# Three steps of the score bound behind each V-projection tile in place of two, in a fused layer norm, attention and feed-forward kernel on eight cores

## The chip, the cores and the metric

The kernel runs on all 8 cores of one Trainium2 chip. Each core takes one half (1024 queries) of the sequence of one of four batch items; the cores don't exchange data. The time is device microseconds of the slowest core. The profile is one execution on the slowest core (core 7).

## The reference

```python
xn = _layernorm(x)                                   # x: (4, 2048, 2048)
# attention on xn: a second layer norm, then
qkv = einsum('bsd,df->bsf', Xn, W_in)                # 16 heads of 128
Q, K = _rope(Q), _rope(K)                            # first 64 channels rotated in pairs
probs = softmax(Q K^T / sqrt(128))
attn = einsum(probs V, W_out) + X
# feed-forward on xn, weights dequantized: (w - 128) * scale
h = silu(xn Wg^T) * (xn Wu^T)                        # 8192 wide
out = x + attn + h Wd^T
```

## The kernel before

The program is a list of operations for each engine, written in the order in which each engine runs them; an operation waits on counters of the operations that it needs. An engine never passes a waiting operation, so the order of the list is the order of the work. There are four stages: layer norms with transposes (`_emit_ln`), attention (`_emit_attention`), output projection, feed-forward.

Attention runs over eight groups `g` of two heads each. In a group, TensorE first makes the projections of Q (4 tiles) and K (8 tiles, each 128x512, 16 matmuls). Behind each of them ACT copies the tile out of its PSUM bank and the rotary embedding of the previous tile follows (`rope`): one matmul into `ppR` (L497) and three DVE operations, a product with the cosine (L501), one with the sine out of PSUM (L505) and their addition (L508). The rotary embedding of the last K tile is left pending and is emitted behind the matmuls of the first V tile.

Then comes the V projection: 16 tiles `tb`, each of 16 matmuls 128x256 (L604), in four PSUM banks in rotation, each copied out by ACT (L611). Beside it the kernel works out, for each head, an upper bound of the scores, which becomes the bias of the exponential. This work is the list `bsteps`, 11 steps a head, 22 a group, in the order

- `s_sq("q",0)`: POOL squares 1024 columns of Q into the buffer `sqb` (L533); it waits for `sq_free`, the last product of the head before,
- `s_mm(0)`, `s_mm(1)`: TensorE sums the squares over the partitions with a matrix of ones (L549) into the bank `j % 3` of S, D0, D1; DVE reduces one row of the bank to its maximum (L555), and the bank is free again behind that (`bankF`),
- `s_sq("k",0)`, `s_mm(2)`, `s_mm(3)`: the same for the first half of K. The square (L538) waits for the last product emitted (`state["mb"]`), since `sqb` is overwritten,
- `s_sq("k",1)`, `s_mm(4)`, `s_mm(5)`: the second half of K,
- `s_fin`: four small DVE operations on the six maxima (L567, L569, L571, L573), a matmul that spreads the value over the partitions (L576), and a copy of it into `biasc` (L579),
- a step that emits nothing and sets `sq_free` for the next head.

Some steps are emitted behind the matmuls of each V tile until the list is empty. Behind the V projection come the loads and POOL casts of the next group's weights (`load_slab`, L444) and then the attention of the group's two heads, whose exponentials wait for `bias_ready` and whose first score matmul waits for the last V tile.

Of the kernel before, what the change touches and what calls it, by code (L numbers as in the profile page):

```python
# [115 lines left out]
def build_program(stage=STAGE, debug=DEBUG):  # L116
# [45 lines left out]
    with ExitStack() as top:  # L162
# [23 lines left out]
        with ExitStack() as sCtx:  # L186
          env["sCtx"] = sCtx
          with ExitStack() as sA:
            env["xn2"] = sA.enter_context(nc.sbuf_tensor("xn2f", [128, ND * S], BF16, side="left"))
            env["cs"] = sA.enter_context(nc.sbuf_tensor("cs_sb", [128, S], F32, side="left"))  # L190
            ldc = []
            for i, (name, dst) in enumerate([
                    ("lnwc", env["lnw"]), ("lnbc", env["lnb"]),
                    ("gscp", env["gsc"]), ("uscp", env["usc"]),
                    ("pmat", env["pm"]), ("idf", env["idf"]),
                    ("cs", env["cs"])]):
                prog.dma("sync", lambda e, d=dst, s=dram[name]: e.dma_start(out=d[:, :], in_=s[:, :]),
                         sem=f"ldc{i}")
                ldc.append((f"ldc{i}", 16))
            env["ldc"] = ldc  # L200
            for dst, valc in [(env["ones_cb"], 1.0), (env["ones_bb"], 1.0), (env["ones_rf"], 1.0),
                              (env["n128"], -128.0), (env["eps_c"], EPS)]:
                prog.op("vector", lambda e, d=dst, vv=valc: e.memset(d[:, :], vv))
            env["dvc_done"] = prog.v("vector")

            _emit_ln(env, xb)
            if debug:
                prog.barrier()
                prog.dma("sync", lambda e: e.dma_start(out=dram["d_xn2"][:, :], in_=env["xn2"][:, :]), sem="st")
                prog.dma("sync", lambda e: e.dma_start(out=dram["d_xnfm"][:, :], in_=env["xnfm"][:, :]), sem="st")  # L210
                prog.dma("sync", lambda e: e.dma_start(out=dram["d_rstd"][:, :], in_=env["rstd"][:, :]), sem="st")
                prog.dma("sync", lambda e: e.dma_start(out=dram["d_nmr"][:, :], in_=env["nmr"][:, :]), sem="st")

            if stage >= 2:
                _emit_attention(env)
                if stage == 2:
                    prog.barrier()
# [167 lines left out]
def _emit_attention(env):  # L385
# [12 lines left out]
    with ExitStack() as ctx:  # L398
# [56 lines left out]
        for g in range(8):  # L455
# [140 lines left out]
            for tb in range(NT):  # L596
                sl = tile_i % 4
                w0 = [("gpsimd", slab_ready[slabv])] + pp_free[sl] + v2_rd
                if g == 0:
                    w0 += env["x2ev"][tb]  # L600
                v2_rd = []
                m_last = None
                for dc in range(ND):
                    m_last = prog.op(T, lambda e, d=dc, t=tb, s=sl, sj=slabv: e.matmul(  # L604
                                         pp4[s][:, 0:256],
                                         xn2f[:, d * S + t * 128: d * S + t * 128 + 128],
                                         wbf[sj % 3][:, d * 256: d * 256 + 256],
                                         start=(d == 0), stop=(d == ND - 1)),
                                     waits=(w0 if dc == 0 else ()))
                wbf_mm_last[slabv % 3] = m_last  # L610
                aev = prog.op(Sc, lambda e, s=sl, t=tb: e.activation(  # L611
                                  v2[:, t * 256:(t + 1) * 256], pp4[s][:, 0:256], AF.Copy),
                              waits=[(T, m_last)])
                vproj_last = aev
                if pending_rope is not None:
                    pending_rope()
                    pending_rope = None
                pp_free[sl] = [(Sc, aev)]
                tile_i += 1
                for _ in range(2):  # L620
                    if bi < len(bsteps):
                        bsteps[bi]()
                        bi += 1
# [554 lines left out]
```

How the kernel before makes its waits and increments, by code:

```python
            def body(eng):  # L89
                for fn, waits, eseq, dsem in ops:
                    if fn == "BARRIER":
                        if e == "sync":
                            eng.sem_inc(sems["bar"], 1)
                        else:
                            eng.drain().then_inc(sems["bar"], 1)
                        eng.wait_ge(sems["bar"], waits)
                        continue
                    for wname, wval in waits:
                        if wname in ENGS:
                            eng.wait_ge(sems["q" + wname], rank[wname][wval])
                        else:
                            eng.wait_ge(sems[wname], wval)
                    inst = fn(eng)
                    if dsem is not None:
                        inst.then_inc(sems[dsem], 16)
                    if eseq in marks:
                        inst.then_inc(sems["q" + e], 1)
```

## Time and profile before

| what | value |
|---|---|
| median of 2 runs | 2918.7 us (2917.88 to 2919.51) |
| profiled execution | 2913.32 us |
| span of the profile, core 7 | 2911.8 us |
| spans of the eight cores | 2901.7 to 2911.8 us |
| mean granted TensorE clock by core | 0.953 to 0.960 |
| V projections of the eight groups | about 291 us to 1267 us, one each 133 to 134 us |

The span runs from the first to the last instruction of a core. PE is TensorE, PEld its weight loads, DVE VectorE, ACT ScalarE, POOL GpSimd. The ends of matmuls are modelled, so the distance between two starts is a better measure than an end. A wait is put down to the operation whose semaphore came last.

### The profile page before, as it was taken

To read this page: it belongs to the slowest core of one execution; us is meant where nothing else is said; L and a number is where in the kernel's file an instruction comes from. 1 tells how busy PE (TensorE), PEld (TensorE's weight loads), DVE (VectorE), ACT (ScalarE), POOL (GpSimd) and SP (SyncE) were. 2 spreads that over 40 slices of the span, in tenths; PEclk is the share of its full clock that TensorE was granted. 3 is DMA by queue.
4 is the path that set the end of the run, shared out by engine and by line. 5 is a ranking of instruction groups with operands and counts; after the bars stand their busy time and mean duration, and the time that the engine had idled before them with its cause. 6 is when DMAs were issued, how large, how long until landed. Compare 5 with 4: busy or idle time off the path is not lost.

```text
span 2911.8 us, 37331 instructions; the slowest of 8 cores (2901.7 to 2911.8 us)
## 1 busy us (share of the span) xinstructions
PE 2590.6 (89%) x12552; PEld 1239.5 (43%) x12552; DVE 633.5 (22%) x1012; ACT 770.8 (26%) x1282; POOL 475.5 (16%) x436
## 2 busy tenths in 40 slices
PE   3537898999999898986979999989998999998996
PEld 2223544445453535442434444434443444443443
DVE  5753352424334342422000000001110000000111
ACT  4572526161625344251111111110001111110000
POOL 2242302121121203000011111110011111110010
PEclk9758999999999999997989999999999999999998
DMA  4113202020211202004133333335544333333553
GB/s 132 59 58 95 87 1 88 1 87 15 74 37 51 62 26 80 1 1 166 66 138 151 145 145 145 145 131 183 182 163 148 148 145 145 145 145 135 186 174 112
DMA packets 64490, 305.61 MB, mean 105 GB/s; under 512 B 7732, under 2 KB 7860, under 8 KB 40632
## 3 DMA queue, kind: packets, MB, share of 16 engines
q1 hardware_dynamic: 55096, 286.45, 27.9%
q10 hardware_dynamic: 9216, 16.78, 1.8%
q8 instruction: 112, 1.84, 0.3%
q14 instruction: 66, 0.54, 0.1%
HBM read 294.81 MB, written 8.39 MB: 104 GB/s over the span
## 4 chain that ended last, share of the span: by engine, by line
PE 85%; DMA 4%; POOL 3%; issue 3%; DVE 3%; ACT 1%; SPq 0%; ACTq 0%; DVEq 0%; POOLq 0%
PE pg L917 15%; PE pu L935 15%; PE pg L990 8%; PE pu L990 8%; PE pp L476 6%; PE ppC L476 6%; PE po L797 4%; PE pp L604 4%; PE ppC L664 4%; PE ppD L672 3%; PE pst L343 3%; PE pp L646 2%; PE ppC L604 2%; POOL sqb L538 2%; PE ppR L497 1%
## 5 line engine op out<-in xcount | busy, mean ns | idle before, releaser
L917 PE MATMUL pg<-xnfm,wstage 128*128 128x512 bf16 x2048 | 465.8, 381 | 18.6 <-ACT sgp L926 12.3
L935 PE MATMUL pu<-xnfm,wstage 128*128 128x512 bf16 x2048 | 464.6, 380 | 2.6 <-DMA wstage<-ubp 2.6
L947 POOL TENSOR_TENSOR hfm<-sgp,sup 128x512 bf16<-128x512 f32 x128 | 161.7, 1264 | 996.2 <-ACT sup L943 996.2
L917 PEld LDWEIGHTS pg<-xnfm,wstage 128*128 128x128 bf16 x2048 | 200.8, 98 | 264.0 <-issue 24.7
L935 PEld LDWEIGHTS pu<-xnfm,wstage 128*128 128x128 bf16 x2048 | 200.8, 98 | 245.7 <-issue 5.3
L926 ACT ACTIVATE sgp<-pg,gsc_sb 128x512 f32<-128x512 f32 x128 | 88.0, 688 | 614.8 <-PE pg L917 344.9
L990 PE MATMUL pg<-wstage,hfm 128*128 128x512 bf16 x1024 | 231.4, 383 | 14.0 <-DMA wstage<-dwp 14.0
L657 ACT ACTIVATE ebig<-pp,biasc 128x512 bf16<-128x512 f32 x344 | 228.7, 687 | 30.3 <-PE pp L646 26.0
L990 PE MATMUL pu<-wstage,hfm 128*128 128x512 bf16 x1024 | 227.7, 379 | 0.0
L967 DVE CAST hsr<-phs 1x512 bf16<-1x512 f32 x2 | 1.4, 679 | 913.0 <-PE phs L956 913.0
L664 PE MATMUL ppC<-ebig,v 128*128 128x512 bf16 x448 | 169.6, 379 | 26.8 <-ACT ebig L657 26.7
L476 PE MATMUL pp<-xn2f,wbf 128*128 128x512 bf16 x768 | 173.9, 381 | 17.1 <-POOL wbf L444 16.8
L943 ACT ACTIVATE sup<-pu,usc_sb 128x512 f32<-128x512 f32 x128 | 88.0, 687 | 373.9 <-PE pu L935 373.9
L697 DVE RECIPROCAL rb<-ppD 128x512 f32<-128x512 f32 x32 | 107.4, 3357 | 351.7 <-PE pp L646 195.8
L343 PE MATMUL pst<-idf_sb,xn2t 128*128 128x128 f32 x256 | 68.8, 365 | 127.1 <-POOL xn2t L320 126.9
L476 PE MATMUL ppC<-xn2f,wbf 128*128 128x512 bf16 x768 | 174.1, 380 | 0.0
L672 PE MATMUL ppD<-ebig,ones_bb 128*128 128x512 bf16 x448 | 169.7, 379 | 0.0
L444 POOL CAST wbf<-wf 128x512 bf16<-128x512 f32 x192 | 118.9, 621 | 250.7 <-DMA wf<-wip 239.7
L990 PEld LDWEIGHTS pg<-wstage,hfm 128*128 128x128 bf16 x1024 | 99.8, 99 | 137.6 <-issue 22.7
L990 PEld LDWEIGHTS pu<-wstage,hfm 128*128 128x128 bf16 x1024 | 98.9, 98 | 120.7 <-issue 3.6
L797 PE MATMUL po<-wob,ctxf 128*128 128x512 bf16 x512 | 113.3, 385 | 28.9 <-DVE wob L781 28.9
L646 PE MATMUL pp<-q,k 128*128 128x512 bf16 x344 | 126.4, 379 | 5.0 <-ACT v L611 5.0
(103 smaller groups left out, 2298.5 us busy)
## 6 DMA issues: line engine op xcount, KB each, us to landing
wstage<-gbp SPq DMA_DIRECT2D x64, 1024.0 KB, 4.9
wstage<-ubp SPq DMA_DIRECT2D x64, 1024.0 KB, 7.0
wstage<-dwp SPq DMA_DIRECT2D x32, 2048.0 KB, 8.9
wf<-wip SPq DMA_DIRECT2D x192, 256.0 KB, 2.9
xt<-xb SPq DMA_DIRECT2D x16, 1024.0 KB, 9.8
wof<-wop SPq DMA_DIRECT2D x8, 2048.0 KB, 9.8
xst<-xb ACTq DMA_DIRECT2D x32, 256.0 KB, 5.3
out<-out_acc ACTq DMA_DIRECT2D x32, 256.0 KB, 3.3
```

What stands on the lines that cost most here:

```text
L343: mm_t = prog.op(T, lambda e, sb=srcbuf, d=dc, pp=p: e.transpose(pp[:, 0:128], sb[:, d * 128:(d + 1) * 128], idf[:, :]), waits=wts)
L476: m_last = prog.op(T, lambda e, d=dc, h=hh, t=tg, s=sl, sj=slabj: e.matmul(pp4[s][:, :], wbf[sj % 3][:, d * 256 + h * 128: d * 256 + (h + ...
L604: m_last = prog.op(T, lambda e, d=dc, t=tb, s=sl, sj=slabv: e.matmul(pp4[s][:, 0:256], xn2f[:, d * S + t * 128: d * S + t * 128 + 128], wb ...
L646: ms_seq[kb] = prog.op(T, lambda e, h=hh, q=qg, k=kb, s=sl: e.matmul(pps[s][:, :], k2[:, h * 2048 + k * 128: h * 2048 + (k + 1) * 128], q2 ...
L657: ex_seq[kb] = prog.op(Sc, lambda e, k=kb, s=sl, h=hh: e.activation(ebig[:, (k % 8) * 512:(k % 8) * 512 + 512], pps[s][:, :], AF.Exp, bias ...
L664: prog.op(T, lambda e, k=kb - 2, h=hh, u=un: e.matmul(ppC[u][:, :], v2[:, k * 256 + h * 128: k * 256 + (h + 1) * 128], ebig[:, (k % 8) * 5 ...
L672: md_seq[kb - 2] = prog.op(T, lambda e, k=kb - 2, u=un: e.matmul(ppD[u][:, :], ones_bb[:, :], ebig[:, (k % 8) * 512:(k % 8) * 512 + 512], ...
L797: m_last = prog.op(T, lambda e, hh=h, t=tb, s=sl, q=wp: e.matmul(po[s][:, :], ctxf[:, hh * 1024 + t * 128: hh * 1024 + (t + 1) * 128], wob ...
L917: m = prog.op(T, lambda e, h=hc, i2=ic2, p=par, t=tg, s=psl: e.matmul(pg[s][:, :], gb2[p][:, h * 256 + i2 * 128: h * 256 + i2 * 128 + 128] ...
L935: m = prog.op(T, lambda e, h=hc, i2=ic2, p=par, t=tg, s=psl: e.matmul(pu[s][:, :], ub2[p][:, h * 256 + i2 * 128: h * 256 + i2 * 128 + 128] ...
L947: gh = prog.op(G, lambda e, i=ic: e.tensor_mul(hfm[:, i * 512:(i + 1) * 512], sgp[:, :], sup[:, :]), waits=[(Sc, a2), (Sc, a1), (T, h_free)])
L990: m = prog.op(T, lambda e, f=fg, p=pc, q=par, t=tb, i=icp: e.matmul(pd[t][:, :], hfm[:, (p * 16 + i) * 512 + t * 128: (p * 16 + i) * 512 + ...
```

## The change

One number: the loop behind each V tile emits up to three steps of `bsteps` in place of two. The steps, their order among themselves and their waits are the same; on every engine they come to stand earlier relative to the V tiles.

```diff
--- before.py
+++ after.py
@@ -617,7 +617,7 @@
                     pending_rope = None
                 pp_free[sl] = [(Sc, aev)]
                 tile_i += 1
-                for _ in range(2):
+                for _ in range(3):
                     if bi < len(bsteps):
                         bsteps[bi]()
                         bi += 1
```

The loop that holds it, with its neighbours:

```python
aev = prog.op(Sc, ... v2[:, t*256:(t+1)*256], pp4[s][:, 0:256], AF.Copy ...)
if pending_rope is not None:
    pending_rope()
    pending_rope = None
pp_free[sl] = [(Sc, aev)]
tile_i += 1
for _ in range(2):            # 3 after the change
    if bi < len(bsteps):
        bsteps[bi]()
        bi += 1
```

## Rows read from the trace of the kernel before

**Rows 1.** The page: busy us (share of the span) and instructions of each engine.

```profile
PE 2590.6 (89%) x12552; PEld 1239.5 (43%) x12552; DVE 633.5 (22%) x1012; ACT 770.8 (26%) x1282; POOL 475.5 (16%) x436
```

**Rows 2.** Waits of PE: waiting line <- releaser: us in total, times, longest.

```profile
PE ppS L576 <- DVE scr L573: 25.3, 16, 2.5
PE ppD L549 <- POOL sqb L538: 16.9, 32, 0.6
```

**Rows 3.** Windows, L604 alone: length, busy us of PE and PEld (x), clock, DMA.

```profile
415.00:470.00 55.00, 29.75 (x256) 24.50 (x256) 1.00 0.16 49
548.00:603.00 55.00, 32.66 (x256) 25.98 (x256) 0.94 0.15 46
...
815.00:870.00 55.00, 31.18 (x256) 25.22 (x256) 0.97 0.14 39
...
sum 440.00, PE 248.60 PEld 201.39; mean PE 31.08 PEld 25.17
```

**Rows 4.** Timeline, PE, third group, behind the long wait for the bias.

```profile
571.57 3.60 PE L604 MATMUL pp<-wbf,xn2f 128*128 128x256 bf16 x16
```

**Rows 5.** Timeline, PE, sixth group: start, us, instruction, [idle before <-releaser].

```profile
961.67 0.39 PE L549 MATMUL ppS<-sqb,ones_bb 128*128 128x512 bf16 x1
...
963.65 0.38 PE L549 MATMUL ppD<-sqb,ones_bb 128*128 128x512 bf16 x1
...
966.32 0.38 PE L549 MATMUL ppD<-sqb,ones_bb 128*128 128x512 bf16 x1 [0.55 <-POOL sqb L538]
966.55 0.38 PE L549 MATMUL ppS<-sqb,ones_bb 128*128 128x512 bf16 x1
...
971.20 0.38 PE L549 MATMUL ppD<-sqb,ones_bb 128*128 128x512 bf16 x1
974.13 0.35 PE L576 MATMUL ppS<-scr,ones_rf 1*128 1x1 f32 x2 [2.55 <-DVE scr L573]
974.41 1.92 PE L604 MATMUL pp<-wbf,xn2f 128*128 128x256 bf16 x16
976.16 1.91 PE L604 MATMUL ppC<-wbf,xn2f 128*128 128x256 bf16 x16
...
985.45 0.61 PE L549 MATMUL ppD<-sqb,ones_bb 128*128 128x512 bf16 x2 [0.55 <-POOL sqb L538]
...
988.46 0.35 PE L576 MATMUL ppS<-scr,ones_rf 1*128 1x1 f32 x2 [0.63 <-DVE scr L573]
988.74 0.50 PE L604 MATMUL ppC<-wbf,xn2f 128*128 128x256 bf16 x3
```

**Rows 6.** Timeline, all engines, second group, end of the first head's steps.

```profile
435.88 0.38 PE L549 MATMUL ppD<-sqb,ones_bb 128*128 128x512 bf16 x1
...
436.40 1.89 POOL L533 TENSOR_TENSOR sqb<-q 128x1024 bf16<-128x1024 bf16 x1 [2.89 <-PE ppD L549]
...
437.64 0.67 DVE L571 TENSOR_TENSOR scr<-scr 1x1 f32<-1x1 f32 x1
```

**Rows 7.** Line L571: duration ns min/median/max, first and last start.

```profile
L571 DVE TENSOR_TENSOR scr<-scr x16: 148/406/666, 304.9 to 1256.9; 1x1 f32<-1x1 f32 x16
```

**Rows 8.** Chain of work that ended last, second group: start, us, what.

```profile
438.56 0.24 issue
```

**Rows 9.** Timeline, all engines, fourth group, around tile 0.

```profile
693.83 0.39 PE L549 MATMUL ppS<-sqb,ones_bb 128*128 128x512 bf16 x1
...
694.01 0.68 DVE L501 TENSOR_TENSOR k<-k,cs_sb 64x512 bf16<-64x512 bf16 x1
...
695.49 0.68 DVE L508 TENSOR_TENSOR k<-k,rb 64x512 bf16<-64x512 bf16 x1
...
696.10 0.67 DVE L555 TENSOR_REDUCE scr<-ppS 1x1 f32<-1x512 f32 x1
```

**Rows 10.** Timelines of POOL and DVE, second group: a square meets a product.

```profile
391.57 1.89 POOL L533 TENSOR_TENSOR sqb<-q 128x1024 bf16<-128x1024 bf16 x1 [30.45 <-DVE q L508]
...
393.09 0.92 DVE L501 TENSOR_TENSOR q<-q,cs_sb 64x512 bf16<-64x512 bf16 x1 [1.72 <-PE ppR L497]
```

## The prediction

> **What bounds the kernel now.** I read the page first: TensorE is busy for 89% of the span and every other engine for less than a third [rows 1]. So time is won or lost where TensorE waits or its clock falls. The change touches only the V projection of each of the eight groups, so I then read the waits of PE. Two entries belong to the interleaved steps [rows 2]: the square products (`s_mm`, L549) wait 32 times for a POOL square, 16.9 us in all, and the bias matmul (`s_fin`, L576) waits 16 times for a chain of small DVE operations, 25.3 us in all. 42 us of 2912 is everything these steps cost as waits. The third view is the windows of the V-projection matmuls group by group [rows 3]: 29.75 us busy where the granted clock is 1.00, up to 32.66 where it fell. The eight groups sum to 248.60, so 248.60 - 8 x 29.75 = 10.6 us go to stretches at the lower of the clock's two levels (1.2 GHz against 2.4), in five of the eight groups (granted clock 0.94 or 0.97 over the window). The timeline of one such group shows where [rows 4]: the tile just behind the long bias wait takes 3.60 us instead of 1.92. The fourth view, the timeline of PE in the sixth group, gives the positions on which I count [rows 5].
>
> **What the change moves.** Nothing is removed or added. There are 22 steps a group (11 a head: q square, two products, k square, two products, k square, two products, fin, close). Two a tile fill tiles 0 to 10; three a tile fill tiles 0 to 7. What can cost is how many V tiles lie between a step and the one that feeds it. I name the products of a head mm0 to mm5 and mark those of the second head with a prime.
>
> Before, by tile: 0 sq mm0; 1 mm1 sq; 2 mm2 mm3; 3 sq mm4; 4 mm5 fin; 5 close sq'; 6 mm0' mm1'; 7 sq' mm2'; 8 mm3' sq'; 9 mm4' mm5'; 10 fin' close.
> After: 0 sq mm0 mm1; 1 sq mm2 mm3; 2 sq mm4 mm5; 3 fin close sq'; 4 mm0' mm1' sq'; 5 mm2' mm3' sq'; 6 mm4' mm5' fin'; 7 close.
>
> A k square is released by a TensorE product, not by its place in TensorE's stream, so the distances are mm1 to mm2 and mm3 to mm4, and they are one V tile before and after, in both heads. This is my first result: the four POOL waits of a group stay. Each is 966.32 - 963.65 = 2.67 us from mm1 to mm2, against 0.22 for the product and 1.75 for the tile (976.16 - 974.41): 0.70 lost [rows 5].
>
> The first q square runs during the Q and K tiles in either version. The second head's waits for mm5 and has two tiles before mm0', before and after.
>
> The bias matmul swaps heads. Before, fin sits right behind mm5 in tile 4 and waits in full: 974.13 - 971.20 = 2.93 us, 2.71 of them lost beyond the product's 0.22. fin' has a tile in front: 988.46 - 985.45 = 3.01 us from mm4', less two products (0.44) and a tile (1.75), 0.8 lost [rows 5]. After, fin has the tile and fin' has none. The second result is that one fin stays naked.
> fin': mm4' to bias again 3.01, less 0.44, is 2.57 lost, 0.14 less than the naked one before.
> fin: here the q square of the second head runs on POOL beside DVE's chain. It starts 0.52 us after mm5 (436.40 - 435.88) and ends at 438.29; the tiny addition L571 starts at 437.64 and ends at 438.31, 0.67 us where the fastest of its kind takes 0.148 [rows 6, 7]. So DVE's addition waits for POOL's square to end. After: mm5 is at 0.22 behind mm4, the square ends at 0.22 + 0.52 + 1.89 = 2.63, the addition at 2.65, the next scalar operation 0.1 + 0.14 later, then 0.25 to TensorE (issue row, [rows 8]): 3.14 from mm4, less 2.19, 0.95 lost.
>
> **The new wait, in tile 0.** mm1 moves from behind tile 1 to directly behind mm0, and the k square with it, into the time in which DVE still works on the last rotary embedding (three operations, `rope`). Let T be the start of mm0, 693.83 [rows 9]. DVE's first rope product runs T+0.18 to T+0.86, the addition `k<-k,rb` (two SBUF inputs) T+1.66 to T+2.34, and the reduction of mm0's bank T+2.27 to T+2.94. Today the square comes after all that (mm1 is at T+1.97, the square 0.5 later). After: mm1 at T+0.22, POOL wants to start at T+0.74. If the first rope product holds it off, T+0.87; it ends at T+2.63 to T+2.76. The addition then meets a running square. Its price is read from another such meeting [rows 10]: POOL's square ends at 393.46, DVE's SBUF-SBUF product ends at 394.01, 0.55 later. So the addition ends at T+3.31 instead of T+2.34, the reduction runs T+3.24 to T+3.91, and mm3, which needs bank S back (`bankF`), may start 0.25 later, at T+4.16. mm2 is ready at T+2.76+0.26 = T+3.02, so mm3 could have been at T+3.24: 0.92 lost, and mm2 itself loses 0.12 more than now. Behind mm3 everything on TensorE queues: tile 2, the next k square, fin. Nothing on another engine is that late that it would hide this. Bounds: if the addition isn't held, mm3 waits only to T+2.94+0.25 = T+3.19 against T+3.12, 0.07 lost; if the reduction were put off by the whole square (1.89 in place of 0.97), 1.9. I take 0.92 because both meetings in the trace show a DVE operation with two SBUF inputs ending with or after POOL's square.
> No row shows the other direction, a POOL square that finds DVE at work; the 0.12 is between nothing and the 0.12 by which the first rope product outlasts T+0.74, and I keep it.
> The Trainium skill, "SBUF — State Buffer", section "Who interferes with whom", has a rule for both directions: a DVE operation with two SBUF inputs and a GpSimd operation that reads SBUF exclude each other, and whichever comes second waits for the whole of the first. By that rule the group comes out at +0.99; with DVE's side of it alone it would be +0.87, and without either at the lower bound. For DVE's side this case's trace agrees (0.67 against 0.148 us [rows 6, 7]); for POOL's side no run here shows it yet.
>
> **Sum of a group at full clock**, from mm0: mm1 0.22; tile 1 0.44 to 2.19; mm2 3.02; mm3 4.16; tile 2 to 6.13; mm4 6.83; mm5 7.05; tile 3 to 9.02; fin 9.97; tile 4 10.25 to 12.00; mm0', mm1', tile 5 12.43 to 14.18; mm2' 14.88; mm3', tile 6 to 17.07; mm4' 17.77; fin' 20.78; tile 7 at 21.06; four tiles later tile 11 at 28.06. Before, the same stretch is 988.74 - 961.67 = 27.07 [rows 5]. Difference +0.99 us a group, +7.9 us for eight. By parts: +0.12 + 0.92 (tile 1) + (0.95 + 2.57) - (2.71 + 0.82) = 1.03, the same within rounding. POOL's casts of the next weights start some 5 us earlier, since the last square is three tiles earlier; nobody waits for them but the next group, so they cost nothing. Bias values are ready earlier too, but their reader, the first exponential of attention, waits for the last V tile.
>
> **The clock.** The naked fin wait stays about as long (2.57 against 2.71 lost) but comes two tiles later and directly behind the wait of mm4'. I leave the 10.6 us as they are. Bounds: 0 if the clock never falls there; 8 x 2.9 = 23.3 if it falls in each group as in the worst one (32.66 - 29.75 = 2.91 [rows 3]), that is -10.6 to +12.7.
>
> Profiled execution: 2913.3 + 7.9 = 2921.2 us, span 2919.7. The median of the runs, 2918.7, lies 5.4 above the profiled execution; I add the sum to the median: 2926.6, rounded 2927.
>
> **Rivals.**
> *No collision on DVE.* The square and the addition pass each other; then the group is 28.06 - 0.12 - 0.85 = 27.09, +0.02, and the change shifts steps without any effect: 2919. For it: the four square waits and one naked fin are unchanged. Against it: [rows 6, 10]. Chance 0.2.
> *The clock stays up.* With mm4 and mm5 in front, the long idle is 0.14 shorter and might spare the low stretches: -10.6 + 7.9 = -2.7, 2916. Against it: this idle comes behind one of 0.7 with only two products between. Chance 0.1.
> *The clock falls in a second place.* After tile 1 TensorE idles twice in quick succession (0.8 before mm2, 0.9 before mm3) with one product between. If that, too, drops the clock, each group pays up to 2.9 more, 23.3 in all, and with the fin' bound 12.7: 2927 + 23 + 13 = 2963, slower, though still by 1.5%. It decides once more than about three groups show a long V tile behind mm3. For 2% it would have to cost 58.4 / 8 = 7.3 us a group, two and a half times the worst group now. Against it: the waits of 0.6 to 0.8 us now never have a slow tile behind them. Chance 0.1; over 2%, 0.01.
>
> **Numbers.** Forecast 0.6. The predicted time is 2927. Low end: no collision and the clock spared, 2919 - 10.6 = 2909. High end: collision, and fin' at its clock bound, 2927 + 13 = 2940. That leaves out most of the second-place rival and a little on either side, less than 2 in 10. A measurement of this kernel can tell some 2% from no change, 58 us, and all cases but an extreme one lie within: faster 0.01, same 0.97, slower 0.02.
>
> **What would show it.** In the changed profile: L538 still releases L549 32 times at about 0.55; the 16 waits of L576 for L573 still sum to about 25, the naked one now in the second head. New: eight waits of L549 (bank S) for DVE L555, about 0.75 each as idle, and eight of the 64 `k<-k,rb` additions at about 1.65 us in place of 0.68. The stretch from mm0 to tile 11 is 28.1 at full clock. If those eight additions stay at 0.68, my new wait is wrong. If the V matmuls' busy sum is far from 248.6, the clock term is.

## The result

| kernel | median of the runs | ratio to before, 95% interval |
|---|---|---|
| before | 2916.1 us | |
| three steps behind each tile | 2921.2 us | 1.0016 [1.0010, 1.0022] |

The change makes the kernel slower by 0.16%, some 5 us, where the prediction had 8 (2927) and a range of 2909 to 2940. The interval leaves out 1, so the difference is clear of the noise; it lies far within the 2% that count as no change. The profile of the changed kernel is of core 6. Its page, the span and the engines' busy time:

```profile
span 2923.7 us, 37114 instructions; the slowest of 8 cores (2901.0 to 2923.7 us)
...
PE 2579.4 (88%) x12335; PEld 1241.6 (42%) x12552; DVE 635.8 (22%) x1012; ACT 770.6 (26%) x1282; POOL 474.9 (16%) x436
```

This trace lacks 217 matmul records (12335 against 12552 [rows 1]; the weight loads are complete), so PE's busy sums can't be compared with those of before. I compare starts instead. The waits of PE, those of the interleaved steps (total us, times, longest):

```profile
PE ppS L576 <- DVE scr L573: 25.5, 16, 2.6
...
PE ppD L549 <- POOL sqb L538: 16.5, 32, 0.6
...
PE ppS L549 <- DVE scr L555: 5.3, 8, 0.8
```

The first two are about what they were, 25.3 and 16.9 [rows 2]. The third is new: once a group, a square product waits for a DVE reduction, 0.66 us each. Of the 64 rotary additions of K, eight on each core (nine on core 0) take 1.53 us or more; the line of L508 (min/median/max ns):

```profile
L508 DVE TENSOR_TENSOR k<-k,rb x64: 682/684/1531, 270.9 to 1237.2; 64x512 bf16<-64x512 bf16 x64
```

The whole of tile 0 to 1 in the fourth group, all engines (compare [rows 9]; the record of mm0 itself, at 700.47 by its weight load, is missing):

```profile
700.65 0.68 DVE L501 TENSOR_TENSOR k<-k,cs_sb 64x512 bf16<-64x512 bf16 x1
700.70 0.38 PE L549 MATMUL ppD<-sqb,ones_bb 128*128 128x512 bf16 x1 [0.16 <-DVE k L508]
...
701.23 1.89 POOL L538 TENSOR_TENSOR sqb<-k 128x1024 bf16<-128x1024 bf16 x1 [33.50 <-PE ppD L549]
...
702.13 1.53 DVE L508 TENSOR_TENSOR k<-k,rb 64x512 bf16<-64x512 bf16 x1
...
703.38 0.38 PE L549 MATMUL ppD<-sqb,ones_bb 128*128 128x512 bf16 x1 [0.55 <-POOL sqb L538]
703.59 0.67 DVE L555 TENSOR_REDUCE scr<-ppS 1x1 f32<-1x512 f32 x1
...
704.41 0.38 PE L549 MATMUL ppS<-sqb,ones_bb 128*128 128x512 bf16 x1 [0.66 <-DVE scr L555]
```

The square runs from 701.23 to 703.12. The rotary addition starts at 702.13 and ends at 703.66, 0.54 after the square; alone it takes 0.68. The reduction of bank S stands behind it, and mm3 (704.41) waits for the reduction. Further down in the same group, PE alone:

```profile
707.08 0.61 PE L549 MATMUL ppD<-sqb,ones_bb 128*128 128x512 bf16 x2 [0.45 <-POOL sqb L538]
707.54 1.91 PE L604 MATMUL ppC<-wbf,xn2f 128*128 128x256 bf16 x16
710.24 0.35 PE L576 MATMUL ppS<-scr,ones_rf 1*128 1x1 f32 x2 [0.79 <-DVE scr L573]
...
718.08 0.61 PE L549 MATMUL ppD<-sqb,ones_bb 128*128 128x512 bf16 x2 [0.53 <-POOL sqb L538]
721.08 0.35 PE L576 MATMUL ppS<-scr,ones_rf 1*128 1x1 f32 x2 [2.40 <-DVE scr L573]
```

The long wait for the bias has moved from the first head to the second and is 0.15 shorter than before (2.55 idle [rows 5]). In this group the clock stays up behind it. In the first group of the same core it falls, and the tiles behind the wait take longer than 1.92 us:

```profile
315.57 0.35 PE L576 MATMUL ppS<-scr,ones_rf 1*128 1x1 f32 x2 [2.40 <-DVE scr L573]
316.02 2.56 PE L604 MATMUL ppC<-wbf,xn2f 128*128 128x256 bf16 x16
318.37 4.71 PE L604 MATMUL pp<-wbf,xn2f 128*128 128x256 bf16 x32
```

For each core I also took from the trace the stretch from mm0 to the first matmul of attention, by the starts of the weight loads, and the time at the clock's lower level in it. Means over the eight cores of the profiled execution, sums over the eight groups:

| kernel | mm0 to attention | of it at the low clock | groups of 64 with low clock | shortest full-clock group |
|---|---|---|---|---|
| before | 302.4 us | 17.9 us | 36 | 36.6 |
| after | 306.5 us | 14.1 us | 23 | 37.4 |

So the eight stretches grew by 4.1 us. Half of the low time is loss (before, a group with 3.4 us of it took some 1.6 us more than one without): the waits added 6.0 us and the clock gave 1.9 back. These 4.1 us are most of the measured 5. In every group of the two traces that has low clock, the low stretch starts between 1.1 us ahead of the bias matmul of the long wait and 1.8 us behind it.

In some executions all cores of one die, or of both, are granted less of the clock and the kernel takes longer; every ratio, and every time in the table of the experiments, is taken from the other runs alone.

### The profile page after: what moved, and what is told of

Same layout as the page of the kernel before. It is cut to its first block, busy times and chain, and to the rows that moved or that the text cites. A ratio compares the mean times of both kernels' runs of the same rounds, so it can differ in the third digit from the quotient of the medians.

```text
span 2923.7 us, 37114 instructions; the slowest of 8 cores (2901.0 to 2923.7 us)
## 1 busy us (share of the span) xinstructions
PE 2579.4 (88%) x12335; PEld 1241.6 (42%) x12552; DVE 635.8 (22%) x1012; ACT 770.6 (26%) x1282; POOL 474.9 (16%) x436
## 4 chain that ended last, share of the span: by engine, by line
PE 83%; issue 4%; DMA 4%; DVE 3%; POOL 3%; ACT 1%; SPq 0%; DVEq 0%; ACTq 0%; POOLq 0%
PE pg L917 15%; PE pu L935 15%; PE pg L990 8%; PE pu L990 8%; PE pp L476 6%; PE ppC L476 6%; PE po L797 4%; PE ppC L664 3%; PE ppD L672 3%; PE ppC L604 3%; PE pp L604 3%; PE pst L343 3%; PE pp L646 2%; POOL sqb L538 1%; PE ppR L646 1%
## 5 line engine op out<-in xcount | busy, mean ns | idle before, releaser
L657 ACT ACTIVATE ebig<-pp,biasc 128x512 bf16<-128x512 f32 x344 | 228.6, 687 | 30.4 <-PE pp L646 21.0
```

Of the source, the lines that this page charges most:

```text
L657: ex_seq[kb] = prog.op(Sc, lambda e, k=kb, s=sl, h=hh: e.activation(ebig[:, (k % 8) * 512:(k % 8) * 512 + 512], pps[s][:, :], AF.Exp, bias ...
```

## The experiments

All ratios are to the kernel before, measured in the same round. In the table "stretch" and "low" are the two sums defined above, for the profiled execution. In after_first and after_fin_first the last rotary matmul lies inside the stretch, eight times 0.33 us (2.6); in the other kernels it lies ahead of it.

| run | median (runs) | ratio, 95% interval | stretch | low |
|---|---|---|---|---|
| after_psum | 2922.0 (9) | 1.0017 [1.0007, 1.0027] | 305.0 | 25.6 |
| before_psum | 2918.1 (7) | 1.0006 [0.9995, 1.0016] | 299.8 | 12.4 |
| early_mm1 | 2913.7 (9) | 0.9993 [0.9982, 1.0004] | 300.6 | 17.9 |
| after_first | 2927.2 (4) | 1.0038 [1.0022, 1.0053] | 317.4 | 38.0 |
| after_fin | 2900.2 (3) | 0.9943 [0.9928, 0.9959] | 286.1 | 0 |
| after_fin_again | 2899.2 (5) | 0.9938 [0.9925, 0.9950] | 286.1 | 0 |
| after_fin_first | 2894.4 (6) | 0.9924 [0.9911, 0.9936] | 286.6 | 0 |
| fin_late_mm1 | 2890.9 (4) | 0.9915 [0.9900, 0.9931] | 279.7 | 0 |
| spread | 2853.0 (3) | 0.9784 [0.9768, 0.9799] | 243.1 | 0 |
| four | 3006.3 (1) | 1.03, one run | 389.0 | 143.8 |


**Does the new wait come from the addition that meets the square?** after_psum takes one of the addition's two SBUF inputs away: the sine product stays in PSUM.

```diff
-    rb[0:64, :], ppR[0:64, :], cs[64:128, t * 512:t * 512 + 512]),
+    ppR[0:64, :], ppR[0:64, :], cs[64:128, t * 512:t * 512 + 512]),
...
-    dd[0:64, do:do + 512], dd[0:64, do:do + 512], rb[0:64, :]),
+    dd[0:64, do:do + 512], dd[0:64, do:do + 512], ppR[0:64, :]),
...
-    ppR_free = [(V, dt2)]
+    ppR_free = [(V, dadd)]
```

> The changed kernel, but the sine product of the rotary embedding stays in PSUM (in place in ppR), so that the addition L508 has one PSUM and one SBUF input. If the new wait comes from the addition being held by POOL's square, the eight additions of 1.53 us go back to 0.68, the wait of L549 for L555 (5.3 us in 8) all but vanishes, a group shrinks by 0.80 - 0.07 us, and the kernel lands within 1 us of the kernel before (ratio 1.000, +0 us against +5 for the changed kernel). If the rival holds (the denser steps as such, or the clock, make the change slower), nothing moves and it stays at 1.0016.

> Control for after_psum: the same edit in the kernel before, where no square runs beside the last addition. Ratio 1.000 (between 0.999 and 1.001) if the edit has no price of its own; the few rotary additions elsewhere that met a square (L508 on q) also go back to 0.68 and gain nothing, since nobody waits for them. If a DVE operation from PSUM were dearer, L508 would show over 0.68 in all 96 places.

The addition in after_psum (min/median/max ns), and the waits of PE:

```profile
L508 DVE TENSOR_TENSOR k<-k,ppR x64: 679/679/680, 271.7 to 1239.3; 64x512 bf16<-64x512 bf16 x64
```

```profile
PE ppS L576 <- DVE scr L573: 25.5, 16, 2.6
...
PE ppD L549 <- POOL sqb L538: 16.0, 31, 0.6
...
PE ppR L497 <- DVE k L508: 4.6, 8, 0.6
...
PE ppD L549 <- DVE scr L555: 0.5, 1, 0.5
```

No addition is held any more, though the square still runs beside it, and the bank-S wait is gone. A full-clock stretch is back at 36.6 to 36.8 us. So the mechanism holds: the same meeting with one input in PSUM costs nothing. The time, however, did not return, and my number was wrong for two reasons. The edit has a price that I had put at nothing: `ppR` is free only after the addition, so the last rotary matmul waits 0.57 us, eight times (the control pays the same 4.6 us). And the low clock rose to 25.6 us. By the total alone this run speaks against the mechanism that its own trace shows. Against its control it speaks for it: from before_psum to after_psum the stretches grow by 5.2 us and the low time by 13.2, half of which is 6.6, so that at equal clock the three steps a tile add nothing; without the edit they added 6.0. The control's ratio of 1.0006 is no sign that the edit is free: its 4.6 us of waits stand against less low clock, 12.4 us in place of 17.9.

**Is the meeting itself the cost, or what stands behind it?** early_mm1 lets them meet but gives mm3 another tile.

```diff
-                for _ in range(2):
+                for _ in range(3 if tb == 0 else 2):
```

> The kernel before with three steps behind tile 0 alone and two behind the others: mm1 and the square meet the last rotary addition as in the changed kernel, but mm3 stands a tile later, and one fin stays naked. If the collision costs only through mm3's wait for bank S, eight additions of L508 are again at 1.53 us, no product waits for L555, the stretch from mm0 to the attention is 36.6 us at full clock as before, ratio 1.000 plus or minus the low clock (0.002). If the collision itself is the cost, it is 37.4 and 1.002.

```profile
L508 DVE TENSOR_TENSOR k<-k,rb x64: 683/683/1530, 270.3 to 1227.6; 64x512 bf16<-64x512 bf16 x64
```

The addition is held for as long as in the changed kernel, nobody on TensorE waits for L555, and the ratio is 0.9993: no cost that the runs can show. This is no clean weighing, for the layout moves other steps too: the shortest full-clock group is 36.2 us, not the 36.6 expected, and the waits for the bias came to 23.6 us in place of 25.3. spread, below, has the same meeting (eight additions of 1.53 us on each core), and there no wait of a step for DVE or POOL is left. The meeting costs only through what needs DVE within the next tile.

**Reductions ahead of the rotary operations.** after_first emits the steps of a tile before the pending rotary embedding.

```diff
-                if pending_rope is not None:
-                    pending_rope()
-                    pending_rope = None
                 pp_free[sl] = [(Sc, aev)]
                 tile_i += 1
                 for _ in range(3):
                     ...
+                if pending_rope is not None:
+                    pending_rope()
+                    pending_rope = None
```

> The changed kernel with the steps of a tile ahead of the pending rotary embedding, so that on DVE the two reductions of tile 0 come before the last addition. If mm3 waits for a reduction that stands behind the held addition, its wait (5.3 us) vanishes; the rotary matmul (0.33 us) also moves into the wait of mm2. 0.80 + 0.33 = 1.13 us a group, 9 us in all at equal low clock: ratio to the kernel before 1.0016 - 0.0031 = 0.9985, and between 0.997 and 1.001 with the low clock. If the wait has another cause, only the 0.33 is won: 1.0007.

My expectation was wrong here. The waits of PE in after_first:

```profile
PE ppS L576 <- DVE scr L573: 25.4, 16, 2.6
...
PE ppD L549 <- POOL sqb L538: 12.3, 24, 0.6
...
PE ppD L549 <- DVE scr L555: 5.3, 8, 0.7
```

The wait is as large as before, but at a D bank instead of S. The timeline of the fourth group, all engines:

```profile
701.18 1.47 DVE L501 TENSOR_TENSOR k<-k,cs_sb 64x512 bf16<-64x512 bf16 x1
...
703.45 2.19 DVE L508 TENSOR_TENSOR k<-k,rb 64x512 bf16<-64x512 bf16 x1
...
706.38 0.38 PE L549 MATMUL ppD<-sqb,ones_bb 128*128 128x512 bf16 x1 [0.66 <-DVE scr L555]
```

Put later, the rotary operations meet two squares: L501 the first (1.47 us), L508 the second (2.19 us). The reduction of mm2 stands behind them, and mm5 waits. I had moved the wait by one tile and lost the clock as well: 38.0 us low, in 62 of 64 groups.

**The long bias wait and the clock.** after_fin puts one empty step ahead of the second head's fin.

```diff
-                                 s_mm(3), s_sq("k", 1), s_mm(4), s_mm(5), s_fin()]
+                                 s_mm(3), s_sq("k", 1), s_mm(4), s_mm(5)] + \
+                                ([lambda: None] if hh == 1 else []) + [s_fin()]
```

> The changed kernel with one empty step ahead of the second head's fin, so that fin' stands behind tile 7 instead of right behind mm5'. The one long bias wait of a group (2.40 us idle) should become about 0.6: 1.75 us a group, 14.0 us in all, off the path. If the low stretches of TensorE's clock in the V projections hang on this wait, they go too (14.1 us of low clock a core, mean of the profile's eight cores, worth half of that, 7 us): ratio to the kernel before 1.0016 - 0.0048 - 0.0024 = 0.9944. If they hang on the sum of the smaller waits, the clock stays as it is: 0.9968.

The waits of PE in after_fin:

```profile
PE ppD L549 <- POOL sqb L538: 16.6, 32, 0.6
...
PE ppS L576 <- DVE scr L573: 11.2, 16, 0.8
...
PE ppS L549 <- DVE scr L555: 5.2, 8, 0.8
```

25.5 became 11.2, and no group of any core has low clock any more. The ratio is 0.9943, as expected from wait and clock together; the 0.9968 expected from the wait alone lies outside the interval. So the low stretches in the V projections hang on the one idle of 2.4 to 2.55 us. The shorter ones, even the pair of 0.55 and 0.66 with one product between, never bring them, which ends the rival of a second place.

> The same swap in the kernel after_fin, whose V projections have no low clock at all, so that the new wait is weighed without it. Against after_fin (0.9943) the collision theory gives 9 us less, 0.9912, and a stretch from mm0 to the attention of 34.9 in place of 35.7 at no low clock. The rival (only the 0.33 us matmul is hidden) gives 2.6 us less, 0.9934.

after_fin_first came to 0.9924, midway between the two numbers. The rotary matmul (0.33 us) now stands in the idle ahead of mm2, which is gone (24 waits for a square of 12.4 us in place of 32 of 16.6), but the wait for L555 stays, at another bank, as in after_first.

**The new wait alone, with the clock silent.** fin_late_mm1 has the distances of after_fin, but mm1 stands behind tile 1.

```diff
-                for _ in range(2):
+                for _ in range({0: 2, 1: 2, 2: 3, 3: 2, 4: 3, 5: 3, 6: 3, 7: 2, 8: 2}.get(tb, 0)):
```

> The same distances as in after_fin (one tile ahead of each k product pair and of both fins), but mm1 behind tile 1 and everything after it one tile later: 2, 2, 3, 2, 3, 3, 3, 2, 2 steps. It differs from after_fin by nothing but the place of mm1, so it weighs the new wait alone, in V projections without low clock. Collision theory: eight fewer waits for L555, L508 back at 0.68, the stretch from mm0 to the attention 35.64 - 0.80 = 34.84 us, 6.4 us in all, ratio to the kernel before 0.9943 - 0.0022 = 0.9921. If the wait for bank S is only a label and TensorE would have waited anyway: 35.64 and 0.9943.

> after_fin once more, beside fin_late_mm1 on the same chip. Both theories: 0.9943 again, 35.64 us from mm0 to the attention, no low clock in the V projections.

The waits of PE in fin_late_mm1; L555 is no longer among them:

```profile
PE ppD L549 <- POOL sqb L538: 16.5, 32, 0.6
...
PE ppS L576 <- DVE scr L573: 11.1, 16, 0.8
```

The additions are back at 0.68 us, but for a few on some cores that meet another operation (here one of 0.77):

```profile
L508 DVE TENSOR_TENSOR k<-k,rb x64: 683/683/769, 270.7 to 1210.2; 64x512 bf16<-64x512 bf16 x64
```

On the same chip and in the same round fin_late_mm1 took 2890.6 to 2894.2 us and after_fin_again 2896.3 to 2899.7. The means are 2891.6 and 2898.3, 6.7 us apart, give or take some 2. In the stretches it is 279.7 against 286.1 us, 6.4, and in the shortest group 34.83 against 35.63. That is the price of the new wait in the clock's absence, 0.80 us a group, and it shows end to end.

**Distances stretched and shrunk.**

In spread two V tiles lie between each release and its use:

```diff
-                for _ in range(2):
+                for _ in range({0: 4, 2: 3, 4: 2, 6: 1, 7: 5, 9: 3, 11: 2, 13: 2}.get(tb, 0)):
```

In four there are four steps behind each tile:

```diff
-                for _ in range(2):
+                for _ in range(4):
```

> The kernel before with the 22 steps laid out so that two V tiles lie between a square's release and its product and between the last product and fin: 4, 3, 2, 1, 5, 3, 2, 2 steps behind tiles 0, 2, 4, 6, 7, 9, 11, 13. By my count all waits of the steps vanish: (4 x 0.70 + 2.71 + 0.82) = 6.3 us a group, 50.6 in all, and the 17.9 us of low clock in the V projections (half of it, 9.0 us): ratio (2916 - 59.6) / 2916 = 0.980. If only the long waits count and the short ones are hidden by TensorE's queue, it is 8 x 2.7 + 9 = 31: 0.989. If distance doesn't matter (the steps' cost is their own work), 1.000.

> The kernel before with four steps behind each tile. The rule of distances (a square needs 2.67 us from release to product, a V tile covers 1.75, a fin directly behind its product 2.71) puts mm4, fin, mm2' and mm4' directly behind what releases them: per group 0.7 (mm2) + 0.8 (bank S) + 2.45 (mm4) + 2.71 (fin) + 2.45 (mm2') + 2.45 (mm4') + 0.8 (fin') = 12.4 us against 6.3, 48 us slower in all, ratio 1.017, and up to 1.025 with more low clock. If it is the number of steps a tile that costs, linearly from 2 to 3 to 4, it is 1.003.

In spread all waits of the steps are gone; what is left of them is a wait for ACT's copy:

```profile
PE ppD L549 <- ACT v L611: 1.3, 8, 0.2
```

The 302.4 us of the stretches are 243.1, each group 30.4 on every core, and the kernel is 2.2% faster than before. The 59.3 us less are the 59.6 forecast, 9.0 of them from the clock. In four:

```profile
PE ppD L549 <- POOL sqb L538: 59.5, 32, 2.4
...
PE ppS L576 <- DVE scr L573: 20.4, 8, 2.5
...
PE ppS L549 <- DVE scr L555: 5.3, 8, 0.8
```

The waits come to 85.2 us against 42.2 before [rows 2], 43 more, near the 48 worked out. The kernel is slower by some 90 us, more than the 1.025 allowed: the low clock in the stretches went from 17.9 to 143.8 us. They grew by 86.7, so about as much again as the waits came from the clock. (Of the 143.8 us, 31.5 fall into the idles, where they cost nothing; half of what is left, less the 17.4 of before, is 47.) With four idles of 2.3 to 2.55 us in a group, three for a square and one for the bias, every group is hit, up to 27 us at the low level. What I had bounded from single falls (2.9 us a group) does not bound repeated ones.

## Why the prediction was right, step by step

**The distances.** Right. The squares' waits (16.9 and 16.5 us) and the sum of the bias waits (25.3 and 25.5) stayed, one fin stayed naked and changed heads. fin behind its tile came to 710.24 - 707.08 = 3.16 us against 3.14 forecast, the naked one to 3.00 against 3.01. spread and four show that the same rule carries to other layouts.

**The new wait.** Right in kind and place: eight waits of bank S, eight additions held. Too large in size: 0.99 us a group with the side of POOL, where the shortest groups differ by 0.80. Two terms were too large. The term of 0.12 us for POOL's square held off by DVE was nothing: the square starts 0.53 after mm1 and mm2 follows mm1 after 2.68, as before (703.38 - 700.70), although DVE's L501 had 0.10 us to run. And mm3 starts 0.15 us behind the reduction, not 0.25; I had taken that step from the bias matmul. Without the two terms the sum gives 0.77.

I also wrote that no row shows POOL held by DVE. That was wrong: the trace of before has it, in the weight casts of the first group. A cast takes 0.61 us alone; the timeline of the kernel before, all engines, has this one:

```profile
268.11 0.68 DVE L501 TENSOR_TENSOR k<-k,cs_sb 64x512 bf16<-64x512 bf16 x1 [1.72 <-PE ppR L497]
268.32 0.95 POOL L444 CAST wbf<-wf 128x512 bf16<-128x512 f32 x1 [1.37 <-DMA wf<-wip]
```

The cast is longer by 0.34 us, while DVE had 0.47 to run at its start. All six casts of this trace that start within such a DVE operation fit: each is longer by what DVE had left, less 0.14 us, and the one with only 0.05 left is not longer. The square's 0.10 lie within that margin. The other direction has the same margin: the rotary operations (0.68 alone) end 0.54 after the square, the tiny L571 (0.148 alone) 0.01 after it. So the held operation ends by its own duration, less 0.14, after the other. The Trainium skill, "SBUF — State Buffer", section "Who interferes with whom", lets the second wait for the whole of the first. The runs agree in both directions, except for these 0.14 us, and by the measurement, not by the rule, the square is not held here. The duration of POOL's instruction, not its start, shows the hold.

**The clock.** I left the 10.6 us as they were. On the mean of the cores it gave back 1.9 us (17.9 to 14.1 us low). That it would hang on the naked fin was right (after_fin). How often it falls for the same wait is not settled: with the long wait in place the kernels had 12.4 (before_psum), 14.1, 17.9, 17.9, 25.6 and 38.0 us of low clock. That is more than the chance of one execution. The spans and mean granted clocks of the cores, over all runs that the ratios use, give an estimate of the low clock of a core in the whole program: 241 us in before_psum, 244 in the changed kernel (26 runs), 250 before (38 runs), 254 in after_psum and 268 in after_first, the same order. In the changed kernel groups 0 to 2 are hit on six of eight cores; in the kernel before the groups differ from core to core. What decides it stays open. This term, some 13 us from end to end when halved, is larger than the effect that was forecast. That it moved by only 2 or 3 us here is luck, since nothing in the prediction fixed it; it is why the total came out at 5, below the 6.0 of the waits. The prediction stood some 3 us higher, half of it by the two terms and the rest by the clock.

The busy sum of the V matmuls, which I had named as the sign for the clock, is no good one: on core 7 of the changed kernel, where the clock never fell there, a group counts 29.27 us, in place of the 29.75 of a full-clock group before.

**The rivals.** No collision: refuted by the additions of 1.53 us and by fin_late_mm1. The clock stays up: true of one core (core 7 had no low clock in these stretches, span 2901.0), not of the slowest. A second place: never seen with three steps (all 23 low stretches lie at the bias matmul); with four steps the clock falls in more places, where the idles are long (in the fourth group of core 1 the tile behind a 2.38 us wait for a square takes 3.09 us in place of 1.92).

## What to carry to other kernels

When small steps are laced into a stream of TensorE tiles, count for each one how many tiles lie between what releases it and what consumes it, and compare with the chain's measured latency; steps per tile say nothing by themselves. Two tiles instead of one hid everything here and gave 2.2%. Look also at which DVE operations with two SBUF inputs run beside a POOL operation, and at what stands behind them in DVE's order.

When an effect is a few microseconds, first take away what makes the clock fall, then weigh it: the removal of the wait could not be seen in the total of after_psum, and in fin_late_mm1 it came out at 6.7 us, where its trace has 6.4.

## What the runs showed of the hardware

- A DVE operation with two SBUF inputs that meets a running POOL operation that reads SBUF ends 0.54 to 0.55 us after it if it is 64x512 (1.53 and 2.19 us in place of 0.68), and 0.01 after it if it is 1x1 (L571, 0.148 alone); with one of the inputs in PSUM it takes 0.68 beside the same square.
- The other way about, POOL's instruction lengthens by what DVE has left, less about 0.14 us (0.95 in place of 0.61). With 0.05 or 0.10 us left it isn't lengthened.
- One idle of TensorE of 2.4 to 2.55 us a group brought 12 to 38 us of low clock a core over the eight groups, each time from within 2 us of that idle's end; idles of up to 0.8 us brought none in any of the 64 groups of after_fin, after_fin_first and fin_late_mm1. Lengths in between were not tried.
